# Moving the exponentials and the row maximum to other places in the first attention of a decoder layer

## The chip, the cores and the metric

The kernel runs on one core of one Trainium2 chip. The metric is the device time of one execution in microseconds (us). The engines are named as the profile names them: PE is the tensor engine's matmul, PEld its weight load, DVE the vector engine, ACT the scalar engine, POOL the GpSimd engine and SP the engine that issues DMAs.

## The reference

One decoder layer runs on 16 sequences of 128 tokens with 256 features. It has three parts, each on a layer norm of `x` and each added to `x`: a differential attention, a cross attention, and a mixture of experts. Only the first is touched by the change, apart from where a wait is written in the second. What it computes is:

```
q = x @ Wq  (16 heads of 128);  k, v = x @ Wk, x @ Wv  (4 heads of 128, each used by 4 query heads)
q, k = rope(q), rope(k)
s1 = q[:64] . k[:64] / 8 ;  s2 = q[64:] . k[64:] / 8          # two maps per head
s1, s2 masked: a query sees its own and the 63 keys before it
a1, a2 = softmax(s1), softmax(s2)
diff = relu(a1 - lam[head] * a2)
diff = diff / (sum(diff) + 1e-6)
x = x + (diff @ v) @ Wo
```

## The kernel before

**Groups, chunks, units.** The first attention is cut into 4 groups of 4 heads (`NG`, one key head each), and within a group into 16 units, one for each sequence (`UN`). A unit computes one sequence for four heads. Four units make a chunk (`c = u // 4`, `j = u % 4` is the unit's place in its chunk), since queries, keys and values are projected for four sequences (512 tokens) at a time. So there are 64 units and 16 chunks. `n = g * UN + u` numbers the units.

**How the order is set.** There is no planner. Each engine has its own `a_unit(g, u, ...)`, which writes that engine's instructions of unit u in a fixed order, and the engines wait for each other's semaphores. Each engine executes its own instructions in the order written. One unit's work is spread over several rounds (a softmax pipeline), so that in round n an engine works on units n, n-1, n-2, n-3 and n-4:

- PE (from L617): slot 0, scores of unit n (L669, 32 small matmuls, semaphore `a_sc`), transposes of the weights of unit n-2 (L683, L685; they wait for `a_dn`), slot 1, weights times values of unit n-2 (L692, called PV here), output projection of unit n-3 (L701, 12 matmuls), slot 2.
- DVE (from L1113): `den` and `rden` of n-2, the addition to `x` of n-4 (L1111), `rec2` and `ratio` of n-1, slot 0, `rho` of n-1, the low part of the output `oal` of n-3 (L1141), the difference of the two maps `a_diff` of n-1 (L1095), the row maximum of n (L1149, L1150, waits for `a_sc`), slot 1, slot 2.
- ACT (from L1461): slot 0, the copy of the transposed weights `pt` of n-2 (L1424), clipping with its row sum, `Relu`, of n-1 (L1501, waits for the difference `a_df`), the eight exponentials of n (L1457, waits for the maximum `a_mx`), slot 1, the copy `oah` of n-2, putting the mask into the score bank.
- POOL (from L1698): the division of the weights by their sum, `a_norm`, of n-2 (L1688).

**Slots.** The projections of the next chunk are spread over a chunk's units in slots. `A_SLOT` gives (place in chunk, slot) for the six items k, q0, q1, q2, v, q3: `{(0,1): k, (1,0): q0, (1,1): q1, (2,1): q2, (3,0): v, (3,1): q3}`. PE projects an item in its slot (L553 for k and the queries, L608 for v), and DVE takes it out with its rope tables in the slot of the same name (`a_take`: L1045 and L1047 for k, L1055 for a query); ACT takes v. All items of this loop go through the one PSUM bank `PJ`. So PE starts an item only when the one before has been taken: it waits for `a_pf`, which DVE's takes raise, and for `a_vf` after v:

```
elif item == AV + 1:
    pe.wait_ge(a_vf, (g_to * NC + c) + 1)
...
else:
    wait(pe, a_pf, (g_to * NC + c) * AW + a_tile(item))
```

The last chunk of the last group has no projections of this kind; slots of its neighbourhood (`A_EXTRA`) hold the layer norm and weight preparation of the cross attention.

**Buffers.** `ea[:, par, m, :]` holds the exponentials of map m of a unit; par is `u % 2`. The first map's place is then overwritten by the difference, by the clipped and by the divided weights, and is read by PE's transposes two rounds later.

Of the kernel before, what the change touches and what calls it, by code (L numbers as in the profile page):

```python
# [16 lines left out]
B, S, DM = 16, 128, 256  # L17
# [4 lines left out]
H, HG = 16, 4  # L22
# [3 lines left out]
QH = S // 2  # L26
SW = HG * S * 3 // 4
# [6 lines left out]
XP = HG // 2  # L34
# [72 lines left out]
def decoder_kernel(nc, x, ctx_in, in_wqk, in_wv, in_wo, in_lam, in_taba, in_rawb, in_tabb, in_kvtab,  # L107
# [8 lines left out]
    def sb(stack, name, shape, dt=f32):  # L116
        return stack.enter_context(nc.sbuf_tensor(name, shape, dt))

    with ctx:
# [20 lines left out]
        negmax = sb(ctx, "negmax", [128, 2, 8])  # L140
        sums = sb(ctx, "sums", [128, 2, 8])
        rec2 = sb(ctx, "rec2", [128, 2, 4])
        ratio = sb(ctx, "ratio", [128, 2, 4])
        rho = sb(ctx, "rho", [128, 2, 4])
        rsum = sb(ctx, "rsum", [128, 2, 4])
        den = sb(ctx, "den", [128, 2, 4])
        rden = sb(ctx, "rden", [128, 2, 4])
        pt = sb(ctx, "pt", [128, 2, HG, S])
# [15 lines left out]
        qab = sb(am, "qab", [128, 2, 2, HG, CW])  # L164
        ea = sb(am, "ea", [128, 2, 2, HG * S])[:, :, :, 0:SW]
        kva = sb(am, "kva", [128, 2, 3, CW])
# [24 lines left out]
        wcol = sb(bm, "wcol", [128, XP, DM], f32r)  # L191
        sb(bm, "b_gap2", [128, 2 * 1024 + 16])
        kvr = sb(bm, "kvr", [128, B, 2, XC])
# [34 lines left out]
        def bank(n):  # L228
            return ps[:, n, :]

        def quads(ap):
            return ap.rearrange("p (h k) -> p h k", k=S)
# [168 lines left out]
        def early(ap):  # L401
            return ap[..., 0:XP * QH].rearrange("... (p k) -> ... p k", k=QH)

        def late(ap):
            return ap[..., XP * QH:SW].rearrange("... (p k) -> ... p k", k=S)

        def a_blocks(ap):
            return [early(ap)[..., p, :] for p in range(XP)] + [late(ap)[..., p, :] for p in range(XP)]
# [138 lines left out]
        def _(pe):  # L547
# [69 lines left out]
            def a_unit(g, u, first=False, final=False, drain=False):  # L617
# [57 lines left out]
                if two:  # L675
                    pe.wait_ge(a_dn, n - 1)
                    wait(pe, a_pt, n - 2)
                    if first and u == 2:
                        pe.wait_ge(ln_h, 2 * 2 + KT)
                    if first and u == 2:  # L680
                        pe.wait_ge(a_ptz, 1)
                    for p in range(XP):
                        pe.transpose(quads(bank(PTB))[0:QH, p, :], early(ea[:, u % 2, 0, :])[:, p, :], idf[:, :])  # L683
                    for p in range(XP):
                        last = pe.transpose(quads(bank(PTB))[:, XP + p, :], late(ea[:, u % 2, 0, :])[:, p, :], idf[:, :])  # L685
                    last.then_inc(a_tp, 1)
# [301 lines left out]
        def _(dve):  # L988
# [103 lines left out]
            def a_diff(n, par):  # L1092
                dve.wait_ge(a_rh, n + 1)
                for h, (e0, e1) in enumerate(zip(a_blocks(ea[:, par, 0, :]), a_blocks(ea[:, par, 1, :]))):
                    last = dve.scalar_tensor_tensor(out=e0, in0=e1, scalar=rho[:, par, h:h + 1], in1=e0,  # L1095
                                                    op0=ALU.mult, op1=ALU.add)
                last.then_inc(a_df, 1)
# [15 lines left out]
            def a_unit(g, u, first=False, final=False, drain=False):  # L1113
# [12 lines left out]
                if two:  # L1126
                    a_den(n - 2, u % 2)
                    a_rden(n - 2, u % 2)
                if not (first and u < 4):
                    add_x((u - 4) % UN, a_wo, n - 4, a_y)  # L1130
                if one:
                    a_rec2(n - 1, (u - 1) % 2)
                    a_ratio(n - 1, (u - 1) % 2)
                slot(0)
                if one:
                    a_rho(n - 1, (u - 1) % 2, g if u else g - 1)
                if not (first and u < 3) and not (drain and u >= 3):
# [5 lines left out]
                if one:  # L1143
                    a_diff(n - 1, (u - 1) % 2)
                if not drain:
                    dve.wait_ge(a_sc, n + 1)
                    wait(dve, a_ex, n - 1)
                    most = negmax[:, u % 2, :].rearrange("p (m h) -> p m h", m=2)
                    dve.tensor_reduce(most[:, :, 0:XP], early(A_S[u % 2]), axis=AX.X, op=ALU.max, negate=True)  # L1149
                    dve.tensor_reduce(most[:, :, XP:HG], late(A_S[u % 2]), axis=AX.X, op=ALU.max, negate=True)\  # L1150
                       .then_inc(a_mx, 1)
                if u == 3 and not drain:
# [269 lines left out]
        def _(act):  # L1422
# [24 lines left out]

            def exps(n, u, maps, mx, ex, free, dst):

                par = u % 2  # L1450
                act.wait_ge(mx, n + 1)
                wait(act, free, n - 1)
                for m in range(maps):
                    for h in range(HG):
                        i = m * HG + h
                        src = a_blocks(A_S[par][:, m, :])[h] if maps == 2 else B_S[:, h // XP, h % XP, :]
                        last = act.activation(dst(m, h), src, ACT.Exp, bias=negmax[:, par, i:i + 1],  # L1457
                                              accum_out=sums[:, par, i:i + 1])
                last.then_inc(ex, 1)

            def a_unit(g, u, first=False, final=False, drain=False):  # L1461
# [29 lines left out]
                if two:  # L1491
                    act.wait_ge(a_tp, n - 1)
                    wait(act, a_pv, n - 3)
                    copy(pt[:, u % 2, :, :], quads(bank(PTB))).then_inc(a_pt, 1)
                if not (first and u < 1) and not (drain and u >= 1):

                    act.wait_ge(a_df, n)
                    par = (u - 1) % 2
                    wait(act, a_dd, n - 2)
                    for h, e in enumerate(a_blocks(ea[:, par, 0, :])):  # L1500
                        last = act.activation(e, e, ACT.Relu, accum_out=rsum[:, par, h:h + 1])  # L1501
                    last.then_inc(a_re, 1)
                if not drain:
                    exps(n, u, 2, a_mx, a_ex, a_tp, lambda m, h: a_blocks(ea[:, u % 2, m, :])[h])
                slot(1)
# [29 lines left out]
            def b_unit(g, u, first=False, final=False, drain=False):  # L1535
# [20 lines left out]
                if not drain:  # L1556
                    exps(n, u, 1, b_mx, b_ex, b_tp, lambda m, h: eb[:, u % 2, h, :])
                slot(1)
# [96 lines left out]
        def _(pool):  # L1655
# [28 lines left out]
            def a_norm(n, par):  # L1684

                pool.wait_ge(a_cb, n + 1)
                for i, part in enumerate((early(ea[:, par, 0, :]), late(ea[:, par, 0, :]))):
                    last = pool.tensor_tensor(part, part, rden[:, par, XP * i:XP * (i + 1)].unsqueeze(2)  # L1688
                                              .broadcast_to([128, XP, (QH, S)[i]]), ALU.mult)
                last.then_inc(a_dn, 1)  # L1690
# [7 lines left out]
            def a_unit(g, u, first=False, final=False, drain=False):  # L1698
                n, c, j = g * UN + u, u // CB, u % CB
                if not (first and u < 2):  # L1700
                    a_norm(n - 2, u % 2)
                if first and u == 2:
# [259 lines left out]
```

## Time and profile before

| what | us |
| --- | --- |
| median of 3 runs (range) | 1332.57 (1331.23 to 1333.62) |
| the profiled execution, its own time | 1330.37 |
| its span | 1328.5 |
| first scores of unit 0 to first scores of unit 63 | 30.0 to 477.7 |
| busy in the span: PE, PEld | 1256.6, 990.3 |
| busy in the span: DVE, ACT, POOL | 836.5, 720.2, 468.3 |
| mean granted TensorE clock, share of 2.4 GHz | 0.991 |

The span is the time from the first to the last instruction of the profiled execution; the execution's own time is 1.9 us longer. Busy time of PE is modelled with matmuls overlapping, so the starts of its instructions say more than their durations. An idle time in brackets behind a row is that of the engine just before the row, with what ended it.

### The profile page before, as it was taken

How to read it: one execution, taken by the hardware profiler on the slowest of the kernel's cores; microseconds unless marked ns; L12 is line 12 of the kernel's file. 1: busy time of each engine (PE TensorE's matmuls, PEld its weight loads, DVE VectorE, ACT ScalarE, POOL GpSimd, SP SyncE). 2: the span in 40 equal slices, each digit the busy share in tenths (PEclk: the TensorE clock that was granted, in tenths of full speed). 3: DMA queues.
4: the chain of work that ended last, by engine and by line, in shares of the span. 5: the costliest groups of instructions: out<-in, count | busy, mean ns of one | idle time of the engine just before them, and what ended most of it. 6: DMA issues, size and time to landing. Idle time of an engine off the chain costs nothing.

```text
span 1328.5 us, 27286 instructions
## 1 busy us (share of the span) xinstructions
PE 1256.6 (95%) x9584; PEld 990.3 (75%) x9584; DVE 836.5 (63%) x1986; ACT 720.2 (54%) x2746; POOL 468.3 (35%) x451
## 2 busy tenths in 40 slices
PE   5799999999999788999999999988999999999998
PEld 4578888888887565666666666567888888888887
DVE  6788888888888676666666656776343443433433
ACT  2788888788888753444444544464332332323322
POOL 3122112212221125454543634641153352533532
PEclk9999999999999989999999999999999999999999
DMA  6002000200012101202103101200335341143340
GB/s 223 17 18 56 18 17 18 57 18 17 17 34 91 33 16 43 82 18 90 35 17 99 25 17 33 76 1 1 111 81 131 63 131 47 39 143 74 57 93 32
DMA packets 34737, 72.78 MB, mean 55 GB/s; under 512 B 7872, under 2 KB 12992, under 8 KB 33344
## 3 DMA queue, kind: packets, MB, share of 16 engines
q1 hardware_dynamic: 34624, 71.32, 20.1%
q8 instruction: 66, 1.08, 0.3%
q14 instruction: 47, 0.39, 0.1%
HBM read 52.29 MB, written 2.23 MB: 41 GB/s over the span
## 4 chain that ended last, share of the span: by engine, by line
PE 74%; DVE 10%; ACT 8%; issue 4%; POOL 2%; DMA 1%; SPq 0%; DVEq 0%; POOLq 0%; ACTq 0%
PE ps L553 33%; PE ps L946 9%; PE ps L669 5%; PE ps L701 4%; PE ps L833 3%; ACT ea L1457 3%; PE ps L739 3%; PE ps L815 3%; PE ps L843 2%; PE ps L692 2%; PE ps L823 2%; PE ps L608 2%; ACT ea L1501 2%; DVE ea L1095 1%; PE ps L683 1%
## 5 line engine op out<-in xcount | busy, mean ns | idle before, releaser
L1830 POOL TENSOR_TENSOR sg<-sg,cw 128x512 f32<-128x512 f32 x88 | 113.8, 1293 | 260.0 <-ACT sg L1620 256.8
L1398 DVE TENSOR_TENSOR hh<-ps,sg 128x512 f32<-128x512 f32 x100 | 69.1, 691 | 178.8 <-POOL sg L1830 161.2
L1424 ACT ACTIVATE hhh<-hh 128x512 fp32r<-128x512 f32 x100 | 63.3, 633 | 213.8 <-DVE hh L1398 211.6
L1457 ACT ACTIVATE ea<-ps,negmax 128x64 f32<-128x64 f32 (+1 forms) x512 | 165.0, 341 | 6.0 <-DVE negmax L1150 6.0
L1424 ACT ACTIVATE pt<-ps 128x512 f32<-128x512 f32 x128 | 77.1, 602 | 165.8 <-PE ps L823 109.6
L1197 DVE TENSOR_TENSOR qcs<-ps,tabb 128x512 f32<-128x512 f32 x192 | 123.5, 685 | 64.6 <-PE ps L553 64.0
L553 PE MATMUL ps<-xnh,wch 128*128 128x512 f32 x400 | 157.3, 393 | 0.0
L553 PE MATMUL ps<-xnl,wch 128*128 128x512 f32 x400 | 157.1, 393 | 0.0
L553 PE MATMUL ps<-xnh,wcl 128*128 128x512 f32 x400 | 155.7, 389 | 0.0
L1688 POOL TENSOR_TENSOR ea<-ea,rden 128x128 f32<-128x128 f32 (+1 forms) x128 | 62.3, 509 | 261.5 <-DVE rden L1106 261.5
L1695 POOL TENSOR_TENSOR eb<-eb,rsum 128x512 f32<-128x512 f32 x64 | 67.1, 1048 | 177.5 <-DVE rsum L1241 177.4
L946 PE MATMUL ps<-wch,hhh 128*128 128x256 f32 x400 | 115.9, 290 | 4.0 <-DVE hhl L1400 2.4
L1400 DVE TENSOR_TENSOR hhl<-hh,hhh 128x512 fp32r<-128x512 f32 x100 | 75.4, 754 | 69.9 <-ACT hhh L1424 69.9
L946 PE MATMUL ps<-wch,hhl 128*128 128x256 f32 x400 | 113.7, 284 | 0.0
L946 PE MATMUL ps<-wcl,hhh 128*128 128x256 f32 x400 | 113.6, 284 | 0.0
L1457 ACT ACTIVATION_READ_ACCUMULATOR ea<-ps,negmax 128x1 f32 x512 | 107.0, 209 | 0.0
L1457 ACT ACTIVATE eb<-ps,negmax 128x128 f32<-128x128 f32 x256 | 90.7, 369 | 26.7 <-DVE negmax L1235 26.4
L669 PEld LDWEIGHTS ps<-kva,qab 128*64 128x64 f32 x2048 | 93.1, 139 | 13.1 <-issue 7.9
L669 PE MATMUL ps<-kva,qab 128*64 128x128 f32 (+1 forms) x2048 | 102.2, 253 | 0.0
L1620 ACT ACTIVATE sg<-ps 128x512 f32<-128x512 f32 x100 | 59.8, 598 | 71.7 <-PE ps L553 71.0
L701 PE MATMUL ps<-woh,oah 128*128 128x256 f32 x256 | 97.5, 381 | 0.7 <-DVE oal L1141 0.7
L1055 DVE TENSOR_TENSOR qab<-ps,taba 128x512 f32<-128x512 f32 x128 | 82.0, 682 | 19.4 <-PE ps L553 19.1
(154 smaller groups left out, 3298.1 us busy)
## 6 DMA issues: line engine op xcount, KB each, us to landing
raw_w<-in_rawb_dram SPq DMA_DIRECT2D x4, 2432.0 KB, 9.0
kva<-ktmp SPq DMA_DIRECT2D x64, 128.0 KB, 2.4
kvt<-qcs SPq DMA_DIRECT2D x64, 128.0 KB, 2.3
cw<-comb_d SPq DMA_DIRECT2D x32, 256.0 KB, 4.9
raw_w<-in_rawc_dram SPq DMA_DIRECT2D x4, 1920.0 KB, 7.9
cw<-comb_d SPq DMA_DIRECT2D x16, 224.0 KB, 4.8
raw_a<-in_wqk_dram SPq DMA_DIRECT2D x4, 768.0 KB, 5.7
cw<-comb_d SPq DMA_DIRECT2D x16, 192.0 KB, 5.6
```

What stands on the lines that cost most here:

```text
L553: last = pe.matmul(out_ap, w, m, start=n == 0, stop=n == len(steps) - 1)
L669: last = pe.matmul(to[rows, h // 2, :], qab[:, c % 2, m, h, S * j + at:S * j + at + QH], kva[:, c % 2, m, S * j:S * j + keys], start=False ...
L701: last = pe.matmul(ps[:, YB, 0:DM], o_[:, (u - 3) % 2, h, :], w_[:, h, :], start=h == 0 and i == 0, stop=h == HG - 1 and i == 2)
L946: last = pe.matmul(ps[:, j // 2, DM * (j % 2):DM * (j % 2 + 1)], h_[:, par, S * j:S * (j + 1)], w_[:, t, 2 * KT * 128:RC_T], start=begin a ...
L1055: last = dve.tensor_tensor(quads(dst), src, bcast(taba[:, tab, :]), ALU.mult)
L1197: last = dve.tensor_tensor(quads(qcs[:, b_at(t), m, :]), quads(bk), bcast(tabb[:, b_table(t), m, :]), ALU.mult)
L1398: dve.tensor_tensor(hh[:, par, :], bank(C_U[par]), sg[:, par, :], ALU.mult).then_inc(c_h, 1)
L1400: dve.tensor_tensor(hhl[:, par, :], hh[:, par, :], hhh[:, par, :].bitcast(f32), ALU.subtract)\
L1424: return act.activation(dst, src, ACT.Copy)
L1457: last = act.activation(dst(m, h), src, ACT.Exp, bias=negmax[:, par, i:i + 1], accum_out=sums[:, par, i:i + 1])
L1695: pool.tensor_tensor(src[:, par, :, :], src[:, par, :, :], rec[:, par, :].unsqueeze(2).broadcast_to([128, HG, S]), ALU.mult).then_inc(done, 1)
L1830: pool.tensor_tensor(sg[:, par, :], sg[:, par, :], cw[:, c % 2, t, :], ALU.mult).then_inc(c_hs, 1)
```

## The change

In the first attention, three things are done.

1. DVE's order within a round: the row maximum of unit n moves from behind the difference to directly behind the addition to `x`. Behind it come `oal`, then `rec2`, `ratio` and `rho` of n-1 in one piece, then slot 0, then the difference.
2. ACT's order: the eight exponentials of unit n go ahead of the clipping of unit n-1.
3. Buffers: `ea` is split into `ea0` (first map) with four buffers and `ea1` (second map) with two; `sums`, `rec2`, `ratio`, `rho`, `rsum`, `den`, `rden` get four buffers too. The exponentials' wait for the transposes goes back one unit further, and they wait for the difference of n-2, which frees `ea1`. The clipping's wait for `a_dd` is gone.

In the cross attention the exponentials have the same waits as before, written outside of `exps`. No instruction of PE or POOL is added, removed or moved, and no DMA. PE's program is row for row the same.

```diff
-        ea = sb(am, "ea", [128, 2, 2, HG * S])[:, :, :, 0:SW]
+        ea0 = sb(am, "ea0", [128, 4, SW])
+        ea1 = sb(am, "ea1", [128, 2, SW])
...
@@ DVE, a_unit
                 if two:
-                    a_den(n - 2, u % 2)
-                    a_rden(n - 2, u % 2)
+                    a_den(n - 2, (u - 2) % 4)
+                    a_rden(n - 2, (u - 2) % 4)
                 if not (first and u < 4):
                     add_x((u - 4) % UN, a_wo, n - 4, a_y)
-                if one:
-                    a_rec2(n - 1, (u - 1) % 2)
-                    a_ratio(n - 1, (u - 1) % 2)
-                slot(0)
-                if one:
-                    a_rho(n - 1, (u - 1) % 2, g if u else g - 1)
-                if not (first and u < 3) and not (drain and u >= 3):
-
-                    dve.wait_ge(a_o, n - 2)
-                    wait(dve, a_wo, n - 4)
-                    dve.tensor_tensor(by_head(oal[:, (u - 3) % 2, :, :]), by_block(bank(OB)),
-                                      by_head(oah[:, (u - 3) % 2, :, :]).bitcast(f32), ALU.subtract).then_inc(a_ol, 1)
-                if one:
-                    a_diff(n - 1, (u - 1) % 2)
                 if not drain:
                     dve.wait_ge(a_sc, n + 1)
                     wait(dve, a_ex, n - 1)
...
                     dve.tensor_reduce(most[:, :, XP:HG], late(A_S[u % 2]), axis=AX.X, op=ALU.max, negate=True)\
                        .then_inc(a_mx, 1)
+                if not (first and u < 3) and not (drain and u >= 3):
+
+                    dve.wait_ge(a_o, n - 2)
+                    wait(dve, a_wo, n - 4)
+                    dve.tensor_tensor(by_head(oal[:, (u - 3) % 2, :, :]), by_block(bank(OB)),
+                                      by_head(oah[:, (u - 3) % 2, :, :]).bitcast(f32), ALU.subtract).then_inc(a_ol, 1)
+                if one:
+                    a_rec2(n - 1, (u - 1) % 4)
+                    a_ratio(n - 1, (u - 1) % 4)
+                    a_rho(n - 1, (u - 1) % 4, g if u else g - 1)
+                slot(0)
+                if one:
+                    a_diff(n - 1, (u - 1) % 4)
...
@@ ACT, a_unit
+                if not drain:
+                    wait(act, a_tp, n - 3)
+                    wait(act, a_df, n - 1)
+                    exps(n, u, 2, a_mx, a_ex, lambda m, h: a_blocks((ea1[:, u % 2, :] if m else ea0[:, u % 4, :]))[h])
                 if not (first and u < 1) and not (drain and u >= 1):
 
                     act.wait_ge(a_df, n)
-                    par = (u - 1) % 2
-                    wait(act, a_dd, n - 2)
-                    for h, e in enumerate(a_blocks(ea[:, par, 0, :])):
+                    par = (u - 1) % 4
+                    for h, e in enumerate(a_blocks(ea0[:, par, :])):
                         last = act.activation(e, e, ACT.Relu, accum_out=rsum[:, par, h:h + 1])
                     last.then_inc(a_re, 1)
-                if not drain:
-                    exps(n, u, 2, a_mx, a_ex, a_tp, lambda m, h: a_blocks(ea[:, u % 2, m, :])[h])
                 slot(1)
```

The vector engine's program in a unit with j = 1 of the first group, kernel before (`rec` is rec2, the two `qab` rows of L1055 behind `ratio` are the take of q0 in slot 0, the `ea` rows are the difference, `negmax` is the row maximum, `a_scores` is raised by PE's scores of this unit):

```order
L1081 RECIPROCAL rec<-sums 128x4 [waits a_exp]
L1085 TENSOR_TENSOR ratio<-rec,sums 128x4 [waits a_rec2]
L1055 TENSOR_TENSOR qab<-ps,taba 128x512 [waits a_projected]
L1055 TENSOR_TENSOR qab<-ps,taba 128x512
L1089 TENSOR_TENSOR rho<-ratio,a_gap 128x4 [waits a_ratio]
L1141 TENSOR_TENSOR oal<-ps,oah 128x2x4x64 [waits a_out,a_o_high]
L1095 SCALAR_TENSOR_TENSOR ea<-ea,rho 128x64 [waits a_rho]
L1095 SCALAR_TENSOR_TENSOR ea<-ea,rho 128x64
L1095 SCALAR_TENSOR_TENSOR ea<-ea,rho 128x128 x2
L1149 TENSOR_REDUCE negmax<-ps 128x2x2 [waits a_exp,a_scores]
L1150 TENSOR_REDUCE negmax<-ps 128x2x2
```

The same place of the vector engine's program in the changed kernel:

```order
L1136 TENSOR_REDUCE negmax<-ps 128x2x2 [waits a_exp,a_scores]
L1137 TENSOR_REDUCE negmax<-ps 128x2x2
L1143 TENSOR_TENSOR oal<-ps,oah 128x2x4x64 [waits a_out,a_o_high]
L1082 RECIPROCAL rec<-sums 128x4 [waits a_exp]
L1086 TENSOR_TENSOR ratio<-rec,sums 128x4 [waits a_rec2]
L1090 TENSOR_TENSOR rho<-ratio,a_gap 128x4 [waits a_ratio]
L1056 TENSOR_TENSOR qab<-ps,taba 128x512 [waits a_projected]
L1056 TENSOR_TENSOR qab<-ps,taba 128x512
L1096 SCALAR_TENSOR_TENSOR ea<-ea,rho 128x64 [waits a_rho]
L1096 SCALAR_TENSOR_TENSOR ea<-ea,rho 128x64
L1096 SCALAR_TENSOR_TENSOR ea<-ea,rho 128x128 x2
```

The wait for the scores moved from the end of this piece to its start, and the take of q0 now stands behind it.

The scalar engine's program in a unit, kernel before (`pt` is the copy of the transposed weights, the `rsum` rows are the clipping, the `sums` rows the exponentials):

```order
L1424 ACTIVATE pt<-ps 128x512 [waits a_pv,a_transposed]
L1501 ACTIVATE ea,rsum<-ea 128x64 [waits a_denominator,a_difference]
L1501 ACTIVATE ea,rsum<-ea 128x64
L1501 ACTIVATE ea,rsum<-ea 128x128 x2
L1457 ACTIVATE ea,sums<-ps,negmax 128x64 [waits a_transposed,a_negmax]
L1457 ACTIVATE ea,sums<-ps,negmax 128x64
```

and in the changed kernel:

```order
L1424 ACTIVATE pt<-ps 128x512 [waits a_pv,a_transposed]
L1456 ACTIVATE ea,sums<-ps,negmax 128x64 [waits a_negmax,a_difference,a_transposed]
L1456 ACTIVATE ea,sums<-ps,negmax 128x64
L1456 ACTIVATE ea,sums<-ps,negmax 128x128 x2
L1456 ACTIVATE ea,sums<-ps,negmax 128x64 x2
L1456 ACTIVATE ea,sums<-ps,negmax 128x128 x2
L1503 ACTIVATE ea,rsum<-ea 128x64 [waits a_difference]
```

The clipping moved behind the eight exponentials; the copy of the transposed weights stays ahead of both.

## Rows read from the trace of the kernel before

**Rows 1.** The page: busy time, share of the span, instructions of each engine.

```profile
PE 1256.6 (95%) x9584; PEld 990.3 (75%) x9584; DVE 836.5 (63%) x1986; ACT 720.2 (54%) x2746; POOL 468.3 (35%) x451
```

**Rows 2.** Timeline, PE, scores of units (start us, us, engine, line, operation, count).

```profile
70.84 1.56 PE L669 MATMUL ps<-kva,qab 128*64 128x128 f32 x32
...
352.54 1.56 PE L669 MATMUL ps<-kva,qab 128*64 128x128 f32 x32
358.24 1.56 PE L669 MATMUL ps<-kva,qab 128*64 128x128 f32 x32
365.63 1.56 PE L669 MATMUL ps<-kva,qab 128*64 128x128 f32 x32
...
378.83 1.56 PE L669 MATMUL ps<-kva,qab 128*64 128x128 f32 x32
...
418.48 1.56 PE L669 MATMUL ps<-kva,qab 128*64 128x128 f32 x32
```

**Rows 3.** Timeline, PE and DVE, around one unit with j = 1 (its scores end at 313.83).

```profile
309.30 1.39 DVE L1047 TENSOR_TENSOR ktmp<-ps,taba 64x512 f32<-64x512 f32 x2
...
310.75 0.19 PEld L553 LDWEIGHTS ps<-xnh,wah 128*128 128x128 f32 x1 [0.22 <-DVE ktmp L1047]
...
312.45 1.29 DVE L1055 TENSOR_TENSOR qab<-ps,taba 128x512 f32<-128x512 f32 x2 [0.36 <-PE ps L553]
...
313.83 0.41 PE L683 MATMUL ps<-idf,ea 128*64 128x128 f32 x2
...
314.21 0.47 PE L553 MATMUL ps<-xnh,wah 128*128 128x512 f32 x1
314.32 1.00 DVE L1095 SCALAR_TENSOR_TENSOR ea<-ea,rho 128x64 f32<-128x64 f32 x4
...
315.24 0.42 DVE L1149 TENSOR_REDUCE negmax<-ps 128x4 f32<-128x256 f32 x1
...
315.68 1.02 PE L692 MATMUL ps<-pt,kva 128*128 128x512 f32 x2
...
316.17 1.28 DVE L1055 TENSOR_TENSOR qab<-ps,taba 128x512 f32<-128x512 f32 x2
```

**Rows 4.** Timeline, DVE, the small steps of one round.

```profile
305.67 0.18 DVE L1081 RECIPROCAL rec<-sums 128x4 f32<-128x4 f32 x1 [0.19 <-ACT ea L1457]
...
306.08 0.16 DVE L1089 TENSOR_TENSOR rho<-ratio,a_gap 128x4 f32<-128x4 f32 x1
306.16 0.69 DVE L1141 TENSOR_TENSOR oal<-ps,oah 128x512 fp32r<-128x512 f32 x1
306.77 0.47 DVE L1095 SCALAR_TENSOR_TENSOR ea<-ea,rho 128x64 f32<-128x64 f32 x2
```

**Rows 5.** Timeline, a maximum for which the vector engine waits for the scores.

```profile
436.85 0.41 PE L683 MATMUL ps<-idf,ea 128*64 128x128 f32 x2
436.97 0.42 DVE L1149 TENSOR_REDUCE negmax<-ps 128x4 f32<-128x256 f32 x1 [1.45 <-PE ps L669]
```

**Rows 6.** Chain that ended last, start us, us: clipping and exponentials of one round.

```profile
248.25 1.16 ACT ea L1501 x8
...
250.15 1.84 ACT ea L1457 x11
```

**Rows 7.** Timeline, PE, idle time before two instructions.

```profile
422.19 0.41 PE L683 MATMUL ps<-idf,ea 128*64 128x128 f32 x2 [2.16 <-POOL ea L1688]
451.74 1.65 PE L712 MATMUL ps<-raw_w 128*128 128x192 f32 x4 [2.61 <-DVE wbl L1204]
```

**Rows 8.** PE by stretches of time: busy, granted clock (PEclk), DMA.

```profile
422.00:426.00 4.00, 3.81 (x22) 1.00 0.87 206
...
448.00:452.00 4.00, 1.39 (x11) 0.95 0.07 12
452.00:456.00 4.00, 3.66 (x36) 0.63 0.02 6
```

**Rows 9.** End of the first attention: busy of PE, PEld, DVE, ACT, POOL, then PEclk.

```profile
418.00:500.00 82.00, 63.72 (x538) 51.56 (x537) 58.02 (x178) 52.15 (x226) 20.44 (x27) 0.94 0.19 57
```

More of the change, by code:

```diff
@@ L140, in decoder_kernel @@
         negmax = sb(ctx, "negmax", [128, 2, 8])
[L141 to L147, printed above, removed]
+        sums = sb(ctx, "sums", [128, 4, 8])
+        rec2 = sb(ctx, "rec2", [128, 4, 4])
+        ratio = sb(ctx, "ratio", [128, 4, 4])
+        rho = sb(ctx, "rho", [128, 4, 4])
+        rsum = sb(ctx, "rsum", [128, 4, 4])
+        den = sb(ctx, "den", [128, 4, 4])
+        rden = sb(ctx, "rden", [128, 4, 4])
         pt = sb(ctx, "pt", [128, 2, HG, S])
@@ L191, in decoder_kernel @@
         wcol = sb(bm, "wcol", [128, XP, DM], f32r)
-        sb(bm, "b_gap2", [128, 2 * 1024 + 16])
+        sb(bm, "b_gap2", [128, 2 * 1024 + 16 + 256])
         kvr = sb(bm, "kvr", [128, B, 2, XC])
@@ L682, in a_unit @@
                     for p in range(XP):
-                        pe.transpose(quads(bank(PTB))[0:QH, p, :], early(ea[:, u % 2, 0, :])[:, p, :], idf[:, :])
+                        pe.transpose(quads(bank(PTB))[0:QH, p, :], early(ea0[:, (u - 2) % 4, :])[:, p, :], idf[:, :])
                     for p in range(XP):
-                        last = pe.transpose(quads(bank(PTB))[:, XP + p, :], late(ea[:, u % 2, 0, :])[:, p, :], idf[:, :])
+                        last = pe.transpose(quads(bank(PTB))[:, XP + p, :], late(ea0[:, (u - 2) % 4, :])[:, p, :], idf[:, :])
                     last.then_inc(a_tp, 1)
@@ L1093, in a_diff @@
                 dve.wait_ge(a_rh, n + 1)
-                for h, (e0, e1) in enumerate(zip(a_blocks(ea[:, par, 0, :]), a_blocks(ea[:, par, 1, :]))):
+                for h, (e0, e1) in enumerate(zip(a_blocks(ea0[:, par, :]), a_blocks(ea1[:, par % 2, :]))):
                     last = dve.scalar_tensor_tensor(out=e0, in0=e1, scalar=rho[:, par, h:h + 1], in1=e0,
@@ L1446, in a_take_v, with exps @@
                 copy(quads(kva[:, c % 2, 2, :]), quads(bank(PJ - AV % turns))).then_inc(a_vf, 1)
-            def exps(n, u, maps, mx, ex, free, dst):
-                par = u % 2
+            def exps(n, u, maps, mx, ex, dst):
+                par, to = u % 2, u % (2 * maps)
                 act.wait_ge(mx, n + 1)
-                wait(act, free, n - 1)
                 for m in range(maps):
@@ L1457, in exps @@
                         last = act.activation(dst(m, h), src, ACT.Exp, bias=negmax[:, par, i:i + 1],
-                                              accum_out=sums[:, par, i:i + 1])
+                                              accum_out=sums[:, to, i:i + 1])
                 last.then_inc(ex, 1)
@@ L1556, in b_unit @@
                 if not drain:
-                    exps(n, u, 1, b_mx, b_ex, b_tp, lambda m, h: eb[:, u % 2, h, :])
+                    wait(act, b_tp, n - 1)
+                    exps(n, u, 1, b_mx, b_ex, lambda m, h: eb[:, u % 2, h, :])
                 slot(1)
@@ L1686, in a_norm @@
                 pool.wait_ge(a_cb, n + 1)
-                for i, part in enumerate((early(ea[:, par, 0, :]), late(ea[:, par, 0, :]))):
+                for i, part in enumerate((early(ea0[:, par, :]), late(ea0[:, par, :]))):
                     last = pool.tensor_tensor(part, part, rden[:, par, XP * i:XP * (i + 1)].unsqueeze(2)
@@ L1700, in a_unit @@
                 if not (first and u < 2):
-                    a_norm(n - 2, u % 2)
+                    a_norm(n - 2, (u - 2) % 4)
                 if first and u == 2:
```

## The prediction

> **What bounds the kernel now.** First the page: PE is busy for 95% of the span, no other engine for more than 75% [rows 1]. So where PE runs without holes, a reorder on DVE or ACT can win nothing; it can only fill holes that PE has, or make new ones. Next the timeline of PE in the first attention, read by the starts of the scores [rows 2]. One chunk of four units goes 5.70 us (352.54 to 358.24), 7.39 (to 365.63), then two units in 13.20 (to 378.83): 26.29 in all. From unit 5 (70.84) to unit 57 (418.48), 13 chunks, the mean is 347.64 / 13 = 26.74, so no chunk has more than a few tenths of avoidable idle time. The place to look for holes is the end of this attention: between 418 and 500 PE is busy for 63.7 of 82 us [rows 9].
>
> Then the waits inside a chunk, DVE beside PE [rows 3]. All projections pass one bank, so PE may not start item i before DVE has taken item i-1. The row at 310.75 shows this wait already biting: PE's weight load for q0 had been idle 0.22 us and was released by DVE's take of k, which ended at 309.30 + 1.39 = 310.69. The take of q0 (312.45 to 313.74) is over before PE wants the bank for q1 at 314.21, 0.38 us after this unit's scores end (313.83, where the transposes start). It is over because, in the order before, this take stands ahead of everything that needs the scores. The margin is 0.47 us.
>
> **The change part by part.** I measure from E, the end of a unit's scores. Where DVE sits waiting, the maximum starts 0.12 us after E (436.85 to 436.97) [rows 5]. After the change DVE does wait there in nearly every unit, since only `den`, `rden` and the addition to x are left ahead of it.
>
> *The take of q0 in a unit with j = 1.* Ahead of it now stand the wait for E and everything behind it. Steps as starts apart: 0.12 until the maximum, maximum 0.93 (315.24 to 316.17) [rows 3], `oal` 0.61 (306.16 to 306.77), `rec2` and `ratio` 0.41 (305.67 to 306.08), `rho` 0.08 [rows 4], then the take itself 1.29 (312.45 row) [rows 3]. Sum 3.44, and 0.06 until PE starts (310.69 to 310.75): PE starts q1 at E + 3.50 where it started at E + 0.38. That is 3.12 us of new idle time on PE, once in every chunk, and nothing hides it, because PE's order is fixed: what stands behind q1 (PV, output projection, next scores) has to wait too.
>
> *The take of q2, ahead of v.* It is in slot 1 of j = 2. Before, `rec2` to the difference were done while PE was still at the scores. Now they follow E: 0.12 + 0.93 + 0.61 + 0.41 + 0.20 for `rho` until the dependent difference (by the step between `rec2` and `ratio`, half of 0.41) + 0.92 for the difference (314.32 to 315.24) + 1.29 = 4.48, + 0.06. PE wants v after transposes and q2 (1.85 from E to PV, 313.83 to 315.68) and some 2.4 us of PV and output projection (what is left of 5.70 when 1.85 and 1.5 of scores are off): E + 4.2. New idle time 0.3.
>
> *The take of k, ahead of q0.* Same chain with k's 2.08 in place of 1.29 (two multiplications in 1.39 [rows 3], and half of that for the third): PE starts q0 at E + 0.12 + 0.93 + 0.61 + 0.61 + 0.92 + 2.08 + 0.06 = E + 5.33. From there a projection (1.47, 314.21 to 315.68) and the scores (1.56 [rows 2]) follow: 8.4 from scores to scores, where it was 7.39. New 1.0.
>
> *The clipping behind the exponentials.* ACT's exponentials of one unit take 2.58 (249.41, which is 248.25 + 1.16, to 251.99), the clipping 1.16 [rows 6]. They could start when the maximum is there, about E + 1.1; ahead of them is the copy `pt`, which waits for PE's transposes and ends at about the same time. So the exponentials start some 1 us earlier than before (the difference no longer stands ahead). But the clipping ends at E + 1.1 + 2.6 + 1.2 = 4.9, and behind it come `den`, `rden` and POOL's division, some 1.5, which makes 6.4: later than the 5.70 at which a short unit's successor wants its transposes. That delay of 0.7 falls in the unit with j = 0, where PE afterwards waits for the take of k anyway, so I cost it at nothing; if it were not covered it would be 0.7 per chunk.
>
> *The buffers and waits.* They remove waits that do not end last anywhere in these rows, and cost no instruction. Nothing.
>
> *Sum.* Per chunk 3.12 + 0.3 + 1.0 = 4.4 us, times 13 chunks = 57. Of the 0.45 by which the mean chunk exceeds 26.29 (5.9 us over 13), the part that already is a wait for a take disappears in the new, longer ones; I take 4 off. Unit 57 has the 3.1 too, but PE waits 2.16 there already [rows 7], which overlaps: +1.3 with its 0.3, so 1. Start and end (unit 1; units 59 to 63, whose slots hold weight preparation that also waits for takes, against ACT's earlier exponentials): between -5 and +6, taken as +3. Subtotal 57 - 4 + 1 + 3 = 57.
>
> *The clock.* PE will now stand idle for 3.1 us some 14 times. In this trace an idle time of 2.16 us left the clock at 1.00 in the stretch behind it [rows 7, 8], and one of 2.61 us was followed by a fall: 0.95 in one stretch of 4 us and 0.63 in the next, so 0.05 x 4 + 0.37 x 4 = 1.7 us of full-speed work lost [rows 7, 8]. Full speed is 2.4 GHz, the lower level 1.2. My 3.1 us is beyond the longer of the two. So the price lies between 0 and 14 x 1.7 = 24 us; with one fall behind a stretch of 2.6 and none behind 2.2, I take it that about two in three fall, and 1.6 each: 15 us. The Trainium skill has a warning that speaks of just this ("TensorE: Matmul & The Clock Gate", section "HAM oscillation — how this bites in real kernels"): a kernel whose tensor engine waits once in each tile can start every tile at the lower clock. That is the upper end as a rule of its own, and a rival below.
>
> Total 57 + 15 = 72 on the profiled execution's 1330.4, so 1402. The median of the runs shown is 2.2 above that execution; the prediction for a median is 1405.
>
> **Rivals.**
>
> *Every stretch falls* (the page's rule taken at its word). Mechanism here: PE idle 3.1 us in j = 1, then q1, PV and the output projection at 1.2 GHz, 14 times. For it: the 2.61 row. Against it: whether a stretch falls seems not to depend on its length alone, since PE is at 1.00 behind 2.16. Time 1332.6 + 57 + 24 = 1414.
>
> *No stretch falls.* Work on both sides of each wait is dense, unlike around 451.74. Time 1332.6 + 57 = 1390.
>
> *Only the wait behind the maximum counts.* If `oal` and the small steps run faster than in the rows or the two smaller waits are absorbed: 14 x 3.1 - 4 = 39, clock unmoved: 1372.
>
> *Faster than before.* The mechanism is ACT's chain at the end of this attention. From 418 to 500 PE is idle for 18.3 us [rows 9]; there each round is ruled by copy, difference, clipping, exponentials on ACT. Taking the difference out of the way of the exponentials in six units gives back up to 1.2 each, 7 us: 1325. It decides if DVE's take of q0 still ends before E + 0.38, which would need it to run ahead of the scores; in the new order it can't, by 3.1 us.
>
> *The change does nothing.* PE is busy for 95%, DVE for 63% and ACT for 54% of the span [rows 1]; with so much slack the two engines might absorb any order. The one-bank wait with a margin of 0.47 us speaks against it. 1332.
>
> **How the numbers follow.** Forecast 0.58 (1405, own range 1394 to 1412); every stretch falls 0.16 (1414); no fall 0.12 (1390); only the one wait 0.06 (1372); more than 1424, by delays that feed on each other, 0.04; faster 0.02; nothing 0.02. The range of 1380 to 1424 leaves out the last four. What a measurement of this kernel can tell from no change is about 0.2%, 2.7 us. Slower by more than that 0.96, within it 0.02, faster 0.02.
>
> **What would show it.** In the changed profile: PE's scores in the middle of the stage some 31 us apart from chunk to chunk without a clock fall, in steps of about 8.8, 7.8, 5.7, 8.4 from j = 1 on; a wait of about 3.1 us of PE's L553 for DVE's query take, 14 to 15 times; DVE's maximum released by PE's scores nearly always; PEclk below 1.00 in many slices between 70 and 480 us; the cross attention and the experts unchanged in length. I am wrong if DVE's query take in j = 1 ends before E + 1, if PE's longest total wait in this stage is for anything else, or if the chunks stay below 28 us.

## The result, and the profile after

| | before | changed |
| --- | --- | --- |
| median, us (range, runs) | 1332.4 (1331.2 to 1333.6, 4) | 1424.2 (1422.1 to 1429.3, 4) |
| profiled execution, its own time, us | 1330.4 | 1429.3 |
| its span, us | 1328.5 | 1427.5 |
| ratio (95% interval) | | 1.0695 (1.0665 to 1.0724) |

The change makes the kernel 6.9% slower. The forecast of 1405 had the direction and the mechanism; the measured median lies just above the range's end of 1424, so the sum was too small, by 19 us of 92. The profiled execution was the slowest of the four; what is worked out from its trace sums to 99, not 92.

The page's line for busy times, which answers to [rows 1]: every engine executes as many instructions as before, in a longer span. PE's busy time is 40 us more for the same instructions, at a mean granted clock of 0.969 where it was 0.991.

```profile
PE 1297.1 (91%) x9584; PEld 1007.0 (71%) x9584; DVE 838.9 (59%) x1986; ACT 723.7 (51%) x2746; POOL 467.3 (33%) x451
```

Next the waits of PE between 80 and 500 us of the changed kernel (engine, what it wanted to do, whom it waited for: total us, times, longest). L1056 is the take of a query, L1048 of k, L1154 the low part of the output weights (`wol`), L1689 the division on POOL, for which the transposes wait.

```profile
PE ps L554 <- DVE qab L1056: 37.4, 13, 3.0
PE ps L554 <- DVE ktmp L1048: 8.2, 12, 0.9
PE ps L702 <- DVE wol L1154: 4.4, 3, 1.5
PE ps L684 <- POOL ea L1689: 3.4, 9, 0.4
```

The first line alone is 13 waits of about 2.9 us, one in each chunk. The other side of the same thing is DVE, whose largest wait in this stretch now is the one for the scores, 50 times:

```profile
DVE negmax L1136 <- PE ps L670: 76.7, 50, 3.8
DVE x_sb L1112 <- PE ps L702: 23.6, 16, 2.2
```

The timeline of one unit with j = 1, which answers to [rows 3]. Its scores end at 380.00, where the transposes start (start us, duration us).

```profile
378.51 1.56 PE L670 MATMUL ps<-kva,qab 128*64 128x128 f32 x32
...
380.00 0.41 PE L684 MATMUL ps<-idf,ea 128*64 128x128 f32 x2
380.12 0.42 DVE L1136 TENSOR_REDUCE negmax<-ps 128x4 f32<-128x256 f32 x1 [1.19 <-PE ps L670]
...
381.06 0.68 DVE L1143 TENSOR_TENSOR oal<-ps,oah 128x512 fp32r<-128x512 f32 x1
381.66 0.17 DVE L1082 RECIPROCAL rec<-sums 128x4 f32<-128x4 f32 x1
...
382.06 0.16 DVE L1090 TENSOR_TENSOR rho<-ratio,a_gap 128x4 f32<-128x4 f32 x1
382.15 1.29 DVE L1056 TENSOR_TENSOR qab<-ps,taba 128x512 f32<-128x512 f32 x2
...
383.50 0.50 PE L554 MATMUL ps<-xnh,wah 128*128 128x512 f32 x1 [2.87 <-DVE qab L1056]
```

The maximum starts 0.12 us behind the scores, the take 2.15 behind them, and PE's next projection at E + 3.50, where the prediction had put it. Before, it was at E + 0.38.

The scores' starts of the same chunk, answering to [rows 2]:

```profile
387.36 1.56 PE L670 MATMUL ps<-kva,qab 128*64 128x128 f32 x32
...
395.34 1.56 PE L670 MATMUL ps<-kva,qab 128*64 128x128 f32 x32
...
401.35 1.56 PE L670 MATMUL ps<-kva,qab 128*64 128x128 f32 x32
...
409.75 1.56 PE L670 MATMUL ps<-kva,qab 128*64 128x128 f32 x32
```

From 378.51 on the four units take 8.85, 7.98, 6.01 and 8.40, together 31.24, where a chunk took 26.29 before. This chunk has no fall of the clock. In ten of the 13 chunks the first of the four steps is longer, 10.4 to 11.7 us, because the clock falls behind the wait. PE in two stretches behind such waits (busy, granted clock, DMA), answering to [rows 8]; the first row of each pair holds the wait (347.79 to 350.66, and the one shown above), the second is the stretch behind it:

```profile
348.00:352.00 4.00, 1.34 (x5) 0.97 0.25 57
352.00:356.00 4.00, 4.00 (x16) 0.60 0.00 0
380.00:384.00 4.00, 1.13 (x10) 1.00 0.44 99
384.00:388.00 4.00, 4.00 (x33) 1.00 0.00 0
```

The same idle time, 2.87 us, is followed by a clock of 0.60 in one case and of 1.00 in the other.

### The profile page after: what moved, and what is told of

Same layout as the page of the kernel before. It is cut to its first block, busy times and chain, and to the rows that moved or that the text cites. A ratio compares the mean times of both kernels' runs of the same rounds, so it can differ in the third digit from the quotient of the medians.

```text
span 1427.5 us, 27192 instructions
## 1 busy us (share of the span) xinstructions
PE 1297.1 (91%) x9584; PEld 1007.0 (71%) x9584; DVE 838.9 (59%) x1986; ACT 723.7 (51%) x2746; POOL 467.3 (33%) x451
## 4 chain that ended last, share of the span: by engine, by line
PE 67%; DVE 21%; issue 5%; ACT 3%; POOL 2%; DMA 1%; SPq 0%; DVEq 0%; POOLq 0%; ACTq 0%
PE ps L554 30%; PE ps L947 9%; PE ps L670 6%; DVE qab L1056 3%; PE ps L740 3%; PE ps L834 3%; DVE negmax L1137 3%; PE ps L702 3%; DVE ea L1096 3%; DVE oal L1143 2%; PE ps L816 2%; PE ps L609 2%; PE ps L844 2%; PE ps L824 2%; PE ps L693 2%
## 5 line engine op out<-in xcount | busy, mean ns | idle before, releaser
L1689 POOL TENSOR_TENSOR ea<-ea,rden 128x128 f32<-128x128 f32 (+1 forms) x128 | 62.0, 505 | 369.0 <-DVE rden L1107 369.0
L554 PE MATMUL ps<-xnh,wah 128*128 128x512 f32 x160 | 74.8, 468 | 55.3 <-DVE qab L1056 40.8
L1456 ACT ACTIVATION_READ_ACCUMULATOR ea<-ps,negmax 128x1 f32 x512 | 111.9, 218 | 0.0
L702 PE MATMUL ps<-woh,oah 128*128 128x256 f32 x256 | 105.6, 412 | 6.5 <-DVE wol L1154 5.9
```

Source lines behind the costliest of these rows:

```text
L554: last = pe.matmul(out_ap, w, m, start=n == 0, stop=n == len(steps) - 1)
L702: last = pe.matmul(ps[:, YB, 0:DM], o_[:, (u - 3) % 2, h, :], w_[:, h, :], start=h == 0 and i == 0, stop=h == HG - 1 and i == 2)
```

## The experiments

The ratios are to the kernel before, timed together with the runs; its medians were 1331.3 (e1, e3, e4), 1330.9 (e5 to e8) and 1331.4 (e9, e10).

| run | median, us | ratio (95% interval) |
| --- | --- | --- |
| e1: changed, slot 0 ahead of the maximum | 1364.2 | 1.0251 (1.0233 to 1.0268) |
| e3: scalar engine's half alone | 1417.6 | 1.0647 (1.0629 to 1.0665) |
| e4: vector engine's half alone | 1441.5 | 1.0834 (1.0816 to 1.0852) |
| e5: changed, PE's wait filled with matmuls | 1406.1 | 1.0563 (1.0545 to 1.0581) |
| e6: order of before, slot 0 behind the maximum | 1375.9 | 1.0332 (1.0315 to 1.0349) |
| e7: exponentials first, maximum just ahead of the difference | 1368.9 | 1.0281 (1.0264 to 1.0299) |
| e8: before, difference ahead of `oal` | 1333.2 | 1.0009 (1.0000 to 1.0019) |
| e9: buffers alone | 1332.6 | 1.0006 (0.9996 to 1.0015) |
| e10: e1 with most of `wol` left out | 1361.6 | 1.0235 (1.0218 to 1.0252) |

**e1: is it the place of slot 0?**

```diff
                     add_x((u - 4) % UN, a_wo, n - 4, a_y)
+                slot(0)
                 if not drain:
                     dve.wait_ge(a_sc, n + 1)
...
                     a_rho(n - 1, (u - 1) % 4, g if u else g - 1)
-                slot(0)
                 if one:
                     a_diff(n - 1, (u - 1) % 4)
```

> The changed kernel with one step put back: the vector engine's slot 0 stands ahead of the row maximum again (directly behind the addition to x), all else as changed. Theory (the new time is mostly the take of q0 standing behind the wait for the scores, with the clock falls that this idle time brings): PE's wait of 2.87 us for the query take vanishes in all chunks and with it the falls, 14 x 3.1 = 44 and about 20 off the changed kernel's 1424: 1360 us, range 1352 to 1368; chunks of about 28.3 us. Rival (everything behind the scores in one serial chain is what holds, whatever step is first): another wait takes its place, the time stays above 1390.

Measured 1364.2, 60 us under the changed kernel. The theory's number was 1360. PE's wait for a query take is gone between 60 and 560 us, but for one of 2.5 at the end of the stage; its largest waits there are:

```profile
PE ps L684 <- POOL ea L1689: 16.6, 27, 2.2
PE ps L554 <- DVE ktmp L1048: 9.5, 14, 0.9
PE ps L702 <- DVE wol L1154: 5.9, 4, 1.5
```

They sum to 32.0 us, and e1 is 32.9 above before. The kernel before has 4.5 us of the first two kinds already (3.3 and 1.2), so these three account for 27.5 of the 32.9. So the place of slot 0 is 60 of the 92 us, and most of the rest is waits that can be named: for the division, for k's take, for `wol`.

**e5: what is the clock's part?** 24 matmuls keep PE at work inside its wait, from unit 5 on; nothing reads their result. The wait ahead of them keeps them behind the addition to `x`, which reads the other half of the same bank.

```diff
                     last.then_inc(a_tp, 1)
+                if j == 1 and not (final and c == NC - 1) and not (first and u < 5) and not drain:
+                    pe.wait_ge(a_y, n - 3)
+                    for _ in range(24):
+                        pe.matmul(ps[:, YB, DM:2 * DM], idb[:, :], maskb[:, 0:DM], start=True, stop=True, skip_group_check=True)
                 slot(1)
```

> The changed kernel with 24 extra bf16 matmuls of 256 columns (about 2.6 us) on PE between transposes and slot 1 in units with j = 1, from unit 5 on; they write the unused half of the output projection's bank, once the addition to x has read the other half, and nobody reads them. They run while PE would wait 2.87 us for the query take, so they delay nothing by more than a few tenths, but PE is not idle. Clock theory: the falls in the middle of the stage vanish (in the trace of the changed kernel the chunks with a fall take 1.6 or 2.8 us longer from the scores of j = 1 to the next, 19.8 us over 13 chunks): 1424 - 20 = 1404, range 1399 to 1410. Rival (the clock costs nothing, the excess comes from elsewhere): 1424 or more.

Measured 1406.1: more work on the busiest engine makes the kernel 18.1 us faster. PE between 80 and 500 us, first before, then the changed kernel, then e5:

```profile
80.00:500.00 420.00, 398.16 (x3640) 0.99 0.12 31
```

```profile
80.00:500.00 420.00, 365.06 (x3108) 0.95 0.08 20
```

```profile
80.00:500.00 420.00, 394.41 (x3571) 1.00 0.11 27
```

The granted clock is back at 1.00, and from unit 5 to unit 53 every unit with j = 1 takes 8.8 to 9.0 us to the next, none 10.4. That shows the clock's price as 18 us at least, about a fifth of the loss. It is some 2 us more, since in unit 57 PE waits only 0.55 for the take in the changed kernel, where the 24 matmuls take 2.78. The Trainium skill's warning ("TensorE: Matmul & The Clock Gate", section "HAM oscillation — how this bites in real kernels"), which the page tells of a kernel with waits of 3 to 5 us, holds here in kind; taken as "every tile" it was too strong, since three of 13 waits had no fall behind them.

**e6: does that one move suffice?** Both engines in the order of before (with the new buffers), slot 0 behind the maximum.

```diff
                 if one:
                     a_rec2(n - 1, (u - 1) % 4)
                     a_ratio(n - 1, (u - 1) % 4)
-                slot(0)
                 if one:
                     a_rho(n - 1, (u - 1) % 4, g if u else g - 1)
...
                     dve.tensor_reduce(most[:, :, XP:HG], late(A_S[u % 2]), axis=AX.X, op=ALU.max, negate=True)\
                        .then_inc(a_mx, 1)
+                slot(0)
```

> The order of before on both engines (with the new buffers), but with the vector engine's slot 0 moved from between ratio and rho to behind the row maximum. Theory (a take that stands behind the scores' maximum is enough by itself): PE waits in each j = 1 for maximum 0.93 and take 1.29, a new wait of about 2.0 to 2.4 us, 14 times, 30 us, with some clock falls 0 to 15: 1367, range 1355 to 1380. Rival (it is harmful only together with the other moves): 1331 to 1340.

Measured 1375.9, 45 above before, in the range and 9 over its middle. PE's waits between 80 and 500 us are mainly one thing:

```profile
PE ps L554 <- DVE qab L1056: 26.4, 13, 2.3
```

That is 2.0 us a time, as expected; the granted clock between 80 and 500 us was 0.96. So a take behind the scores' maximum is enough by itself.

The clock falls here too, behind shorter waits. Two of them, of the same length, with a stretch behind each (busy, granted clock, DMA):

```profile
165.31 0.50 PE L554 MATMUL ps<-xnh,wah 128*128 128x512 f32 x1 [1.76 <-DVE qab L1056]
166.00:170.00 4.00, 4.00 (x14) 0.57 0.00 0
195.26 0.50 PE L554 MATMUL ps<-xnh,wah 128*128 128x512 f32 x1 [1.76 <-DVE qab L1056]
196.00:200.00 4.00, 4.00 (x38) 1.00 0.00 0
```

From unit 5 to unit 53 nine of the 13 waits, which are 1.76 to 2.34 us long, have a fall behind them. Each fall makes the step to the next scores about 1.6 us longer, 14.6 in all; with 26.2 of waits this makes 41 of the 45 us. The prediction had read from [rows 7, 8] that a wait of 2.2 us leaves the clock alone; e6 shows that it need not.

**e3 and e4: the two halves.** e3 has ACT's new order and DVE's old one, e4 the reverse. e3 as a difference to the changed kernel (DVE):

```diff
                     add_x((u - 4) % UN, a_wo, n - 4, a_y)
-                (row maximum)
-                (oal)
-                (rec2, ratio, rho)
-                slot(0)
-                (difference)
+                (rec2, ratio)
+                slot(0)
+                (rho)
+                (oal)
+                (difference)
+                (row maximum)
```

> The scalar engine's half of the change and the buffers alone: exponentials ahead of the clipping, but the vector engine in the order of before. Theory (the vector engine's order is the cause): no wait for a query take; only the later clipping can bite, through POOL's division, as a wait of PE's transposes of 1 to 2 us in short units: 1345, range 1333 to 1360. Rival (exponentials ahead of the clipping are themselves a cause): above 1370.

Measured 1417.6. Here my theory fell: I had expected 1345, and the prediction had costed the later clipping at nothing. The timeline of e3 shows what I had not seen:

```profile
315.64 0.41 DVE L1150 TENSOR_REDUCE negmax<-ps 128x4 f32<-128x256 f32 x1
315.97 0.67 DVE L1151 TENSOR_REDUCE negmax<-ps 128x4 f32<-128x512 f32 x1
316.68 0.31 ACT L1457 ACTIVATE ea<-ps,negmax 128x64 f32<-128x64 f32 x1 [0.84 <-DVE negmax L1151]
...
319.22 0.29 ACT L1504 ACTIVATE ea<-ea 128x64 f32<-128x64 f32 x1
...
320.45 0.16 DVE L1102 SCALAR_TENSOR_TENSOR den<-sums,rsum 128x4 f32<-128x4 f32 x1 [1.35 <-ACT ea L1504]
...
323.45 0.42 DVE L1150 TENSOR_REDUCE negmax<-ps 128x4 f32<-128x256 f32 x1
```

It is a closed loop. The maximum releases the exponentials (316.68), behind them comes the clipping (319.22), for which `den` waits (320.45), and `den` stands first on DVE: the next maximum comes only behind it and all else, at 323.45, where this one was at 315.64. 7.8 us for one round, where PE needs 5.7 or 7.4. In the kernel before, the clipping was ahead of the exponentials, so `den` had long been released.

e4 is the changed kernel with ACT's two blocks the other way round:

```diff
+                (clipping, L1503)
                 (exponentials)
-                (clipping, L1503)
                 slot(1)
```

> The vector engine's half of the change and the buffers alone: maximum first, slot 0 behind it, but on the scalar engine the clipping ahead of the exponentials as before. Theory: the full wait for the query take stays (about 3 us, 14 times) and now the clipping, which needs the difference at the end of the vector engine's chain, holds back the exponentials: at least as slow as the changed kernel, about 1440, range 1424 to 1475. Rival (the two halves hurt separately and add up): about midway, 1380.

Measured 1441.5; expected about 1440. So neither half is a gain, and they don't add up: 86 and 110 alone, 92 together. My reading of the two orders, which no run takes apart: with the maximum early the closed loop is short; with the exponentials first the late difference holds back less.

**e7: the maximum just ahead of the difference.** The closed loop as a theory, put to a test of its own: `rec2`, `ratio`, slot 0, `rho`, `oal` as before, then maximum, then difference; ACT as changed.

```diff
                     a_rho(n - 1, (u - 1) % 4, g if u else g - 1)
                 (oal)
-                (difference)
                 (row maximum)
+                (difference)
```

> The change taken by its words: exponentials ahead of the clipping, the maximum just ahead of the difference, everything else of the vector engine in the order of before (slot 0 between ratio and rho). New theory after the scalar half alone gave 1418: with the exponentials ahead, a closed loop arises: exponentials 2.6, clipping 1.2, den, rden and addition 0.8 (they stand first on the vector engine and wait for the clipping), then all that stands ahead of the maximum (rec2 to oal 1.2, slot 0 1.3 where it is full), maximum 0.9, exponentials again: 6.9 us in a unit without a full slot 0 and 8.2 with one, against PE's 5.7 and 7.4. It gives 28 to 29 per chunk: 1370, range 1355 to 1385. Rival (only takes behind the scores matter): 1330 to 1340.

Measured 1368.9, expected 1370. No take stands behind the maximum in a slot 0 here; PE's waits in the stretch from 80 to 500 us are for the division instead, 25 times:

```profile
DVE den L1102 <- ACT ea L1504: 74.0, 53, 1.9
...
PE ps L684 <- POOL ea L1690: 29.1, 25, 2.2
```

**e9: the buffers alone.** The order of before on both engines, with `ea0`, `ea1` and the small buffers of the change; as a diff it is the change's buffer lines alone.

> Both engines in the order of before, with the split and enlarged buffers (ea0 four, ea1 two, sums and the small ones four) and their waits. Theory: the buffers neither give nor cost anything: 1331, range 1328 to 1334. Rival (the new places in memory or the extra wait cost something that is hidden in the sum): above 1336.

Measured 1332.6, ratio 1.0006 (0.9996 to 1.0015): nothing, as predicted. (The exponentials' wait for the transposes goes back by two units, from n-2 to n-4, and not by one as the description of the change says.)

**e10: the wait for `wol`.**

```diff
+                    dm = DM if first else 8
-                    dve.tensor_tensor(wol[:, :, :], wo[:, bass.ds(g * HG, HG), :], woh[:, :, :].bitcast(f32),
+                    dve.tensor_tensor(wol[:, :, 0:dm], wo[:, bass.ds(g * HG, HG), 0:dm], woh[:, :, 0:dm].bitcast(f32),
```

> The kernel of run e1 (changed kernel, slot 0 ahead of the maximum), in which the low part of the output weights (wol, computed once per group at unit 3 on the vector engine, about 1.3 us behind the difference) is computed for 8 of 256 columns in groups 1 to 3; this leaves out most of that subtraction. Theory (in the new order the subtraction ends too late for the output projection, a wait of 1.47 us in each group that the prediction did not have): 3 x 1.47 = 4.4 us below e1's 1364.2: 1360, range 1358 to 1361. Rival (another wait, for oal, ends just as late): 1364.

Measured 1361.6 (1359.4 to 1364.3) against e1's 1364.2 (1362.8 to 1365.5): the two ranges overlap, so the times alone don't settle it. The traces do in part: PE's wait for `wol` fell from the 5.9 us shown for e1 to

```profile
PE ps L702 <- DVE wol L1155: 2.8, 4, 1.5
```

of which 1.5 is group 0's, left as it was. 3.1 us gone, not 4.4. What is left is some 0.4 a time, and the trace puts it down to the small `wol` itself, which still stands behind the difference, and not to `oal` as the rival had it:

```profile
177.05 0.18 DVE L1155 TENSOR_TENSOR wol<-raw_w,woh 128x32 fp32r<-128x32 f32 x1
177.29 0.39 PE L702 MATMUL ps<-woh,oah 128*128 128x256 f32 x1 [0.43 <-DVE wol L1155]
```

**e8: a try for a kernel that beats both.**

```diff
+                if one:
+                    a_diff(n - 1, (u - 1) % 2)
                 if not (first and u < 3) and not (drain and u >= 3):
...
                                       by_head(oah[:, (u - 3) % 2, :, :]).bitcast(f32), ALU.subtract).then_inc(a_ol, 1)
-                if one:
-                    a_diff(n - 1, (u - 1) % 2)
```

> The kernel before with one exchange on the vector engine: the difference ahead of oal. Try for a kernel that beats both. The difference, and behind it clipping and exponentials, come 0.5 us earlier in every unit; oal comes 0.9 later but has 1.9 us until PE wants it. PE has almost nothing to gain in the middle (0.45 per chunk), some in the last six units: 1328, range 1324 to 1333, same within the noise in one case of three. Rival (oal then delays PV): slower, up to 1345.

Measured 1333.2, ratio 1.0009, where I had expected 1328: no gain that can be measured, and if anything a loss. Four waits of PE's PV for `oal`, 2.0 us in all, are new. None of the runs beats the kernel before.

## Why the prediction was right in kind and short in size

The mechanism stood; the step that failed is the sum. It left out two things that now come late on DVE and for which PE waits: the take of q3, ahead of the next chunk's first scores (0.3 us a chunk), and `wol` (1.5 a group). And it took the clock, and with it the start and end, too small.

**Right: the one-bank wait.** The prediction read it off a 0.22 us wait that was already there and a margin of 0.47. PE starts q1 at E + 3.50, predicted and measured. e1 takes it away alone and e6 puts it in alone; both move the time as it should.

**Right: which unit costs what.** From j = 1 on: 8.8, 7.8, 5.7, 8.4 predicted, 8.85, 7.98, 6.01, 8.40 measured. That is 4.95 a chunk where the sum had 4.4. Two terms are short. The step with v, from j = 2 to j = 3, is 0.48 longer, not 0.3: before, PE started v 4.13 us behind the scores (346.53 to 350.66), not 4.2, and from v to the next scores it now takes 1.98 where it took 1.88. And from j = 3 to j = 0 the sum had nothing, where the step went from 5.70 to 6.01. The first scores of a chunk need all its queries; q3's take, in slot 1 of j = 3, stands behind the difference, which has become late, and so ends only just before them:

```profile
400.01 1.29 DVE L1056 TENSOR_TENSOR qab<-ps,taba 128x512 f32<-128x512 f32 x2
401.35 1.42 PEld L670 LDWEIGHTS ps<-kva,qab 128*64 128x64 f32 x32 [0.32 <-DVE qab L1056]
```

PE's weight loads wait for it ten times between 80 and 500 us, 3.1 in all; before, the scores never waited for a query take there. In the three other chunks the wait for `wol` covers it. Over 13 chunks the two terms are 7 us.

**Missed: the low output weights.** Once in a group `wol` is computed behind the difference, which had become late. PE's output projection then waits 1.5. From unit 5 to 57 it falls in three units (7.56 where the others have 6.00), 4.7 us. In the kernel before, the same units took 6.01 to 6.19 in place of 5.70. That may have been a clue, though no wait for `wol` is named there.

**Mis-sized: the clock.** 15 us were set for 14 waits, with bounds of 0 and 24. The profiled execution's 13 chunks carry 19.8 (the sum of what their first steps have over 8.85, nearly all in ten of them, three of these with 2.7 to 2.9). Unit 57 carries 3 more: PE waits 2.17 for the division there, as before, and then 0.55 for the take, and its step is 11.64 where it was 7.96. The stretches behind these two waits:

```profile
512.00:516.00 4.00, 3.45 (x10) 0.52 0.99 224
516.00:520.00 4.00, 4.00 (x17) 0.62 0.96 413
```

So the profile has 23, and e5, with the 2 us that its filling costs in unit 57, gives 20 for the medians. "Two in three fall, 1.6 each" was nearly right on the count and low on the size, since a fall can last twice as long.

**Mis-sized in part: start and end.** They were taken as 3, and unit 57's wait as 1. Unit 57's 0.55 was in order, and the units 58 to 63 take 51.6 where they took 51.3. From unit 0 to unit 5 the profiled execution has 5.7 more, and behind unit 63 5.3 more. But not all of this is the change's. From the first scores of unit 0 to those of unit 1 the changed kernel has 11.55 us, and e5, whose program up to there is the same, has 8.38; e9, with the order of before, has 11.38. PE from 32 to 40 us, in the changed kernel, e5 and e9:

```profile
32.00:40.00 8.00, 5.81 (x21) 0.71 0.00 1
```

```profile
32.00:40.00 8.00, 5.81 (x54) 1.00 0.00 1
```

```profile
32.00:40.00 8.00, 5.81 (x18) 0.71 0.00 1
```

The clock there differs from execution to execution, whatever the order, and it makes 3.2 of the 5.7. The rest is the new waits (PE waits 2.8 for a query take in its second unit, where I took the waits for data to hide it). Behind unit 63 it is the clock again. PE in the 79 us from the last unit's scores on, first before, then changed:

```profile
478.00:557.00 79.00, 71.03 (x547) 0.98 0.17 53
```

```profile
571.00:650.00 79.00, 69.92 (x508) 0.94 0.18 53
```

The granted clock is 0.04 lower for 79 us, which is 3 us of full-speed work. e8 and e9 have 0.96 in the same 79 us, and 852.9 and 852.8 us behind unit 63 where the profiled execution of before has 850.8. So 2 of the 5.3 are that execution's, not the change's. The rest I did not take apart.

The sum of the profiled execution: 13 chunks x 4.95 = 64, clock 23, `wol` 5, less 4 for waits of before that the new ones cover, unit 57's wait 1, start 5, end 5: 99, against 98.9 measured. Without the 3.2 and the 2.0 that are not the change's, and with e5's 20 for the clock, it is 91, against 92 for the medians. Against the forecast's 72 the misses are 7 for the chunks' waits, 5 for `wol`, 5 for the clock and some 3 for start and end.

**Right in this order only: the late clipping at no cost.** The delay came in the unit with j = 0 and was covered by the wait for k, as argued: the transposes wait 0.34 for the division, and q0 starts at E + 5.32, predicted 5.33.

```profile
403.25 0.41 PE L684 MATMUL ps<-idf,ea 128*64 128x128 f32 x2 [0.34 <-POOL ea L1689]
```

But the prediction did not see the closed loop. e3 shows that the clipping behind the exponentials costs 86 us when the maximum stays where it was; the early maximum is what keeps that from the changed kernel. And where slot 0 is put right, e1 has 16.6 us of waits for the division, the largest part of what keeps it from the kernel before.

**The rivals.** "Every stretch falls" had 1414 and "no stretch falls" 1390; the clock's part was between, nearer to the first. "Only the wait behind the maximum" (1372) is out by the 8.2 us of waits for k and by e5, which shows that the clock has a price. "Faster" and "nothing" are out.

## What to carry to other kernels

An instruction that waits for the busiest engine should stand on its helper behind everything that the busiest engine will want next: ask of each move not what it lets start earlier, but what now queues behind its wait. When an in-order loop runs over two engines, write down the closed loop of releases and add it up before and after; an exchange that looks local can put the whole length of one engine's round into it, and two exchanges can each be bad alone. And a wait of the tensor engine costs more than its length: here 2.9 us came with 1.4 more on the average, and filling it with idle matmuls gave that back.

## What the runs showed of the hardware

The same wait of 2.87 us was followed by the lower clock (0.60 in the stretch from 352 to 356 us) in one chunk and by full clock in another. Ten of 13 such waits had a fall behind them, three none. Three of the ten cost 2.7 to 2.9 us and the other seven 1.6 to 1.7, where the one fall of [rows 8] had cost 1.7. In e6 waits of 1.76 to 2.34 us had a fall behind them nine times in 13, about 1.6 us each, and waits of 1.76 us stand in both groups. Between 32 and 40 us the same instructions ran at a clock of 0.71 in two executions (changed, e9) and at 1.00 in a third (e5).
